# One attention block of three tokens split into two, and the orders of five engines rewritten from the first window sum up to the router

## The chip, the cores and the metric

One core of a Trainium2 chip runs the program. Its engines are TensorE (PE in the profile, with its weight loads as PEld), VectorE (DVE), ScalarE (ACT), GpSimd (POOL) and SyncE (SP), each with its own instruction stream, in order, tied by semaphores. The metric is device time in microseconds (us) of one execution, the median of several.

## What is computed

All in float32. An image tokenizer, an attention layer over 6 tokens, and a mixture of 8 experts with 2 picked for each token, for 64 images:

```python
pe = conv(pixels, conv_w)                     # 6 x 6 patches of 14 x 14 pixels per image, 256 channels
red, win = mean of each 3 x 3 window, its 9 patches      # 4 windows per image
q = ln(red) @ la_wq;  k, v = ln(win) @ la_wkv            # 8 heads of 32, 9 keys each
local = red + softmax(q k) v @ la_proj + la_proj_b       # 4 rows per image
gq = ln(class_emb) @ ga_wq;  gk, gv = ln(local) @ ga_wkv
cls_out = class_emb + softmax(gq gk) gv @ ga_proj + ga_proj_b
h = concat([cls_tok, local @ mod_w + mod_b, cls_out])    # 6 tokens per image: 0, 1 to 4, 5
x = layernorm(h)
h = h + causal_attention(x @ Wq, x @ Wk, x @ Wv) @ Wp + bp   # 16 heads, alibi distances
x = layernorm(h)
logits = x @ gate_w; the two largest, their softmax weights
h = h + sum over both picks of weight * (silu(x @ gate) * (x @ up)) @ down
```

Token i attends to the tokens j <= i, so the attention has 1 + 2 + 3 + 4 + 5 + 6 = 21 pairs.

## The kernel before

The program is one straight order on each engine, written out by hand; what an engine issues waits for semaphores of the others, and everything behind it on that engine waits too.

*The front.* Convolution, window attention (`window_scores`, `score_maximum`, `window_exp`, `window_weights`, `value_products` on two halves wt = 0 and 1). The weighted values of half 0 lie in `vprod` as three groups; `vsum_step` counts the two additions by which GpSimd (L1745) sums them, and `first_aggregate` transposes the sum into `agg0`. Half 1 is summed by TensorE itself in `second_aggregate` (`summed_turn`, L798). `local_rows`, `local_copy`, `local_columns` and `copy_pair` make the `loT` columns of each half.

*From the columns to h.* For each half, `patch_begin` and `patch_rows` (L839, L845) form the rows of h of tokens 1 and 2 (tile 0) and 3 and 4 (tile 1). `global_scores`, a softmax on DVE (L2121 to L2134), `global_value`, `gprod` (L2137), `global_aggregate` (L872), `gaggT` (L2142), `class_begin` and `class_rows` (L886) form those of tile 2, tokens 0 and 5. Each tile's rows get moments (DVE), a reciprocal root (GpSimd, `reciprocal_root`, L1638), the normalised rows `in0`, `in1`, `in2`, a transposition (`turn_in`, L661), a copy to `hT` (ACT), and the products with Wq, Wk, Wv (`qkv`, L958): `qkv_cls` is token 0, `qkv0` tokens 1 and 2, `qkv1` tokens 3 and 4, `qkv_pool` token 5. ACT unpacks each of the four in four copies (`qkv_copy`, L1444 to L1447). h itself is copied to `acc` by ACT (`h_copy`, L1356), and GpSimd adds the bias (`residual`, L1740).

*The token attention.* DVE works in blocks of query tokens (`BLOCKS`): all their query-key products (L517), the sum to scores (`att_dots`, L2062), maximum and difference (`att_scores`), exp on ACT (`attention_exp`, L1452), and sum, reciprocal and product (`att_weights`). A block of queries i0 to i1 works on (i1 - i0) x i1 pairs, masked ones too: 9 and 18, in all 27. `token_values` (L508) multiplies weights and values: GpSimd does tokens 1, 2 and 0, and the keys 0 and 1 of tokens 5 and 3; DVE does the other keys of 5 and 3, and token 4. TensorE transposes and sums (`turn_context`, L798): `ctx0` is tokens 1, 2, 0, `ctx1` tokens 3 and 4, `ctx2` token 5. ACT copies them (L1457), and `out_proj` (L981) adds the product with Wp to h in the banks of the three row tiles.

*Up to the router.* For each tile: moments (`residual_moments`), root, `mid_normalise` (DVE), `turn_mid`, a rounded copy by ACT (`experts_input_hi`, L1463), the rest by DVE (`experts_input_lo`, L2092), and `router`, six matmuls each. `logits_full` is set behind the last. `keep_clock` issues matmuls whose result nobody reads.

*Behind it.* The dense expert (`gate_up`, L1076; `down`, L1086), the picks and the places of the rows (DVE, L2176 to L2259), rows scattered to DRAM and read back, and 11 tiles of 128 rows for the other experts (L1148, L1157, L1171). Expert weights are split in a high and a low part: `weights_hi` and `weights_lo` (GpSimd, L1696) for the dense one, `tile_weights_hi` (L1471) and `tile_weights_lo` (DVE, L2098) in four pieces for each tile. SP loads the second tile's weights (`tile_a(1)`) over the buffers of q, k, v, once all token values are done.

## Time and profile before

| | |
|---|---|
| median of 3 runs | 201.01 us (200.23 to 202.35) |
| the profiled execution | 200.45 us, its span 198.6 us, granted TensorE clock 1.000 |
| busy share of the span | PE 93%, PEld 81%, DVE 70%, ACT 53%, POOL 38% |
| from the window values of half 1 to the logits | 81.5 us to 119.4 us after the span's start |
| from the logits to the last matmul | 119.4 us to 194.5 us |

The span runs from the first to the last instruction. A matmul of float32 operands stands as two in the counts.

### The profile page before, as it was taken

What the parts mean: (1) busy time and instruction counts of PE and PEld (TensorE: products, weight loads), DVE (VectorE), ACT (ScalarE), POOL (GpSimd) and SP (SyncE); (2) the same over time, 40 slices, a digit from 0 to 9 for tenths busy, and PEclk for the clock granted to TensorE, in tenths of its full rate; (3) what the DMA queues carried; (4) which work ended last, traced back from release to release, by engine and by line L of the source; (5) the groups of instructions that cost most, each with busy time, mean ns of one, the idle gap of its engine ahead of it and who ended that gap; (6) DMA issues with size and microseconds to landing.
All of it is one profiled execution on the core that took longest, in us unless ns stands there. A gap on an engine that the chain in (4) does not pass through costs nothing.

```text
span 198.6 us, 3342 instructions
## 1 busy us (share of the span) xinstructions
PE 184.0 (93%) x1093; PEld 160.7 (81%) x1093; DVE 138.6 (70%) x334; ACT 104.8 (53%) x234; POOL 75.2 (38%) x110
## 2 busy tenths in 40 slices
PE   8499999999999999999994879999999999999991
PEld 8499798989798778867892769988888888888880
DVE  1379778095899999857388867938657866766452
ACT  4255477183434646525653254247367877778331
POOL 6105548165635322038835472781000022000770
PEclk9999999999999999999999999999999999999999
DMA  6999999500087000000000490033899999994233
GB/s 193 301 344 337 325 370 317 152 2 0 5 310 323 0 0 3 0 0 2 3 0 0 145 386 0 2 106 93 294 373 381 406 383 373 347 356 147 70 93 79
DMA packets 11933, 34.88 MB, mean 176 GB/s; under 512 B 1462, under 2 KB 7180, under 8 KB 10252
## 3 DMA queue, kind: packets, MB, share of 16 engines
q1 hardware_dynamic: 9436, 30.72, 43.8%
q10 hardware_dynamic: 1904, 2.37, 3.9%
q0 software_dynamic: 576, 1.58, 2.4%
q8 instruction: 9, 0.15, 0.3%
q14 instruction: 8, 0.07, 0.1%
HBM read 30.84 MB, written 3.82 MB: 174 GB/s over the span
## 4 chain that ended last, share of the span: by engine, by line
PE 63%; DVE 22%; issue 4%; DMA 4%; ACT 2%; SPq 2%; POOL 0%; DVEq 0%
PE bank L1148 15%; PE bank L1171 9%; PE bank L616 8%; PE bank L714 4%; PE bank L1076 4%; DMA raw<-xb 4%; PE bank L637 3%; PE bank L1086 3%; PE bank L661 2%; DVE kv_rows L1856 2%; DVE stats L1809 2%; PE bank L1157 2%; DVE vprod L496 2%; SPq L491 1%; DVE window L508 1%
## 5 line engine op out<-in xcount | busy, mean ns | idle before, releaser
L1148 PE MATMUL bank<-split 128*128 128x512 f32 x132 | 33.3, 401 | 0.1
L1148 PEld LDWEIGHTS bank<-split 128*128 128x128 f32 x132 | 24.0, 188 | 5.2 <-DVE split L2270 0.3
L1638 POOL TENSOR_TENSOR rstd<-veps,mhalf 128x1 f32<-128x1 f32 (+2 forms) x17 | 14.3, 842 | 27.7 <-DVE veps L1816 27.6
L616 PE MATMUL bank<-split 128*128 128x256 f32 (+1 forms) x180 | 22.7, 285 | 0.0
L616 PEld LDWEIGHTS bank<-split 128*128 128x128 f32 (+1 forms) x180 | 22.1, 191 | 0.2
L714 PE MATMUL bank<-split 128*128 128x512 f32 x90 | 22.1, 397 | 0.0
L2098 DVE TENSOR_TENSOR split<-raw,split 128x512 fp32r<-128x512 f32 x28 | 18.1, 685 | 4.2 <-ACT split L1471 4.1
L714 PEld LDWEIGHTS bank<-split 128*128 128x128 f32 x90 | 16.4, 188 | 3.3
L1471 ACT CAST split<-raw 128x512 fp32r<-128x512 f32 x28 | 16.6, 619 | 1.8 <-DMA raw<-ffn_w 1.8
L1658 POOL TENSOR_TENSOR window<-window,pe_rows 128x256 f32<-128x256 f32 x14 | 13.3, 951 | 9.0 <-ACT pe_rows L1246 8.3
L1734 POOL TENSOR_SCALAR split<-token_row,window 128x384 fp32r<-128x384 f32 x3 | 4.0, 1349 | 30.7 <-DMA window<-expert_rows 30.7
L2279 DVE TENSOR_TENSOR kv_rows<-bank,kv_rows 128x512 f32<-128x512 f32 x11 | 7.6, 690 | 11.5 <-PE bank L1148 9.5
L637 PE MATMUL bank<-split 128*128 128x256 f32 (+1 forms) x90 | 12.0, 289 | 2.8 <-ACT split L1261 2.8
L1246 ACT COPY pe_rows<-bank 128x256 f32<-128x256 f32 x18 | 6.3, 370 | 15.4 <-PE bank L616 15.4
L1297 ACT ACTIVATE kv_rows<-bank,rstd 128x512 f32<-128x512 f32 x15 | 10.0, 686 | 7.5 <-PE bank L714 6.6
L637 PEld LDWEIGHTS bank<-split 128*128 128x128 f32 (+1 forms) x90 | 11.3, 195 | 3.2 <-ACT split L1261 2.8
...
L2098 DVE TENSOR_TENSOR split<-kv_rows,split 128x512 fp32r<-128x512 f32 x16 | 10.5, 695 | 2.6 <-ACT split L1471 2.6
L1809 DVE BATCH_NORM_STATS2 stats<-pe_rows 128x6 f32<-128x256 f32 x18 | 6.5, 414 | 8.3 <-ACT pe_rows L1246 8.1
L1261 ACT CAST split<-raw 128x384 fp32r<-128x384 f32 (+1 forms) x15 | 6.7, 510 | 8.9 <-DMA raw<-xa 4.6
L1471 ACT CAST split<-kv_rows 128x512 fp32r<-128x512 f32 x16 | 9.5, 620 | 1.4 <-DMA kv_rows<-ffn_w 1.4
L1547 ACT ACTIVATE kv_rows<-bank 128x512 f32<-128x512 f32 x11 | 6.6, 597 | 5.5 <-PE bank L1148 5.5
...
## 6 DMA issues: line engine op xcount, KB each, us to landing
...
```

The source lines that it names most:

```text
L616: mm = pe.matmul(bank[b][:, 0:C], xs[0:n, g % 2, px, a:a + P], cws[0:n, pw, k, :], start=(k == 0 and m == 0), stop=(k == len(KCH) - 1 and ...
L637: mm = pe.matmul(bank[GT * g + j][:, 0:C], xs[0:n, g, px, a:a + P], cws[0:n, pw, k, :], start=(k == 0 and m == 0), stop=last)
L714: mm = pe.matmul(bank[b][:, :], lns[:, g % 2, px, a:a + P], wkvs[:, pw, aw:aw + 2 * C], start=(c == 0 and m == 0), stop=(c == CC - 1 and m ...
L1076: mm = pe.matmul(bank[b][:, 0:NCOL], aws[:, q, pw, a:a + P], ms[:, px, c, FIRST:ROWS], start=(c == 0 and m == 0), stop=(c == CC - 1 and m ...
L1148: mm = pe.matmul(bank[half][:, :], xst[:, s % 2, px, c * P:(c + 1) * P], tile_aws[s % 2][:, piece, pw, :], start=(c == 0 and m == 0), stop ...
L1171: mm = pe.matmul(bank[6][:, 0:C], hcols[s % 2][:, q * P:(q + 1) * P], b_ring[ring(s)][:, q, :], start=(q == 0), stop=(q == FQ - 1))
L1297: act.activation(kv_rows[:, 0:wt + 2:wt + 1, n, :], bank[b][:, :].rearrange("p (k c) -> p k c", k=2), ACT.Identity, scale=rstd[:, k, i - G ...
L1471: act.copy(tile_aws[s % 2][:, piece, HI, :].rearrange("p (q n) -> p q n", q=FQ), a_ring[ring(s)][:, :, piece * P:(piece + 1) * P]).then_in ...
L1638: pool.tensor_tensor(rstd[0:parts, k, 0:n], veps[0:parts, k, 0:n], mhalf[0:parts, 0:n], ALU.pow).then_inc(rstd_done, 1)
L1658: pool.tensor_tensor(redsum[:, wt, :], pe_rows[:, wt, 0, :] if n == 1 else redsum[:, wt, :], pe_rows[:, wt, n, :], ALU.add).then_inc(sum_s ...
L1809: ins = dve.bn_stats(stats[0:parts, j, :], r)
L2098: dve.tensor_tensor(tile_aws[s % 2][:, piece, LO, :].rearrange("p (q n) -> p q n", q=FQ), a_ring[ring(s)][:, :, piece * P:(piece + 1) * P] ...
```

## The change

The attention block of tokens 3, 4 and 5 becomes one of tokens 3 and 4 and one of token 5; all values of tokens 3, 4 and 5 go to DVE. The order of each engine is rewritten: GpSimd's sum of `vprod` goes, TensorE sums the three groups while it transposes; `qkv_cls` is multiplied and copied there, in bank 6 in place of bank 3; `last_keys` goes ahead of `class_keys`; tile 0's rows of h come right behind `local_rows(1)`; DVE adds bias and h (`residual`), in place of an ACT copy and a GpSimd addition; GpSimd's `weights_lo` go elsewhere; `qkv0` and `qkv1` are begun a token at a time; the token values are transposed in the order 4, 5, 3, with `out_proj(2)` between; `router(0)` goes ahead of `turn_mid(1)`; two of DVE's `tile_weights_lo(0, ...)` go behind the last rows, one ahead of and one behind the routing.

The diff, with its lines of context and the declarations of semaphores left out:

```diff
@@ -60,12 +60,11 @@
-BLOCKS = [(0, 3), (3, 6)]
+BLOCKS = [(0, 3), (3, 5), (5, 6)]
 PAIRS = PAIR_AT[-1]
-SHARE = 2
@@ -91,7 +90,7 @@
-QKV = {"qkv_cls": (3, (0,)), "qkv0": (0, (1, 2)), "qkv1": (1, (3, 4)), "qkv_pool": (4, (5,))}
+QKV = {"qkv_cls": (6, (0,)), "qkv0": (0, (1, 2)), "qkv1": (1, (3, 4)), "qkv_pool": (4, (5,))}
@@ -141,10 +140,10 @@
                                                     "loT0", "loT1", "in0", "in1", "in2"],
-    ["conv3", "turn0", "turn1", "turn2", "q0", "turn3", "turn4", "turn5", "gs", "qkv_cls", "ctx0", "mid0"],
+    ["conv3", "turn0", "turn1", "turn2", "q0", "turn3", "turn4", "turn5", "gs", "ctx0", "mid0"],
     ["conv5"] + [f"kv{i}" for i in range(1, TILES, KV_BANKS)] + ["wp2"],
-    ["bv"] + [f"kv{i}" for i in range(2, TILES, KV_BANKS)] + ["wp0"],
+    ["bv"] + [f"kv{i}" for i in range(2, TILES, KV_BANKS)] + ["qkv_cls", "wp0"],
...
@@ -500,14 +499,13 @@
-def token_values(eng, i, j0=0, j1=None):
-    j1 = i + 1 if j1 is None else j1
+def token_values(eng, i):
     x = PAIR_AT[k] + (i - i0) * i1
-    return eng.tensor_tensor(pv[:, pv_at[i] + j0:pv_at[i] + j1, :].rearrange("p j (h e) -> p j h e", e=DV),
-                             v6[:, j0:j1, :, :].rearrange("p j a (g e) -> p j (a g) e", e=DV),
-                             spread(p6[:, x + j0:x + j1, :], 3, DV), ALU.mult)
+    return eng.tensor_tensor(pv[:, pv_at[i]:pv_at[i + 1], :].rearrange("p j (h e) -> p j h e", e=DV),
+                             v6[:, 0:i + 1, :, :].rearrange("p j a (g e) -> p j (a g) e", e=DV),
+                             spread(p6[:, x:x + i + 1, :], 3, DV), ALU.mult)
@@ -557,7 +555,7 @@
         if s == 1:
-            sp.wait_ge(pool_values, BLOCKS[0][1] + 2)
+            sp.wait_ge(pool_values, BLOCKS[0][1])
@@ -787,15 +785,35 @@
+    def qkv(name, part=None):
+        b, tokens = QKV[name]
+        wait_free(pe, b, name)
+        w = QW + KW + VW
+        for n, t in enumerate(tokens):
+            if part in (None, n):
+                for c in range(CC):
+                    mm = pe.matmul(bank[b][:, n * w:(n + 1) * w], hT[:, t, c, :, :].rearrange("p s b -> p (s b)"),
+                                   wqkv[:, c, :], start=(c == 0), stop=(c == CC - 1))
+        if part in (None, len(tokens) - 1):
+            mm.then_inc(filled[b], 1)
+    def summed_turn(out, piece, first, last):
+        return pe.matmul(out, piece, ident, start=first, stop=last, is_transpose=True)
-        pe.wait_ge(vsum_step, 2)
-        for c in range(CC):
-            turn(c, "agg0", [vprod[:, 0, c * P:(c + 1) * P]])
-    def summed_turn(out, piece, first, last):
-        return pe.matmul(out, piece, ident, start=first, stop=last, is_transpose=True)
+        pe.wait_ge(vprod_step, VSTEPS)
+        for c in range(CC):
+            wait_free(pe, c, "agg0")
+            for n in range(GT):
+                mm = summed_turn(bank[c][:, 0:P], vprod[:, n, c * P:(c + 1) * P], n == 0, n == GT - 1)
+            mm.then_inc(filled[c], 1)
+            if c == 0:
+                pe.wait_ge(att_in, 16)
+                pe.wait_ge(tok_cols, 1)
+                qkv("qkv_cls")
@@ -809,7 +827,7 @@
             if k == 0:
-                global_scores(0)
+                local_begin(1)
@@ -890,6 +908,8 @@
         pe.wait_ge(residual_done, ROW_ORDER.index(j) + 1)
+        if j == 2:
+            pe.wait_ge(class_residual, 1)
@@ -933,8 +953,8 @@
     keys_values(GT * 4 + 2)
+    last_keys()
     class_keys()
-    last_keys()
@@ -947,29 +967,22 @@
-    def qkv(name, part=None):
-        b, tokens = QKV[name]
-        wait_free(pe, b, name)
-        w = QW + KW + VW
-        for n, t in enumerate(tokens):
-            if part in (None, n):
-                for c in range(CC):
-                    mm = pe.matmul(bank[b][:, n * w:(n + 1) * w], hT[:, t, c, :, :].rearrange("p s b -> p (s b)"),
-                                   wqkv[:, c, :], start=(c == 0), stop=(c == CC - 1))
-        if part in (None, len(tokens) - 1):
-            mm.then_inc(filled[b], 1)
+    def turn_values(k, b, n):
+        t = CTX_TOKENS[k][n]
+        for j in range(t + 1):
+            mm = summed_turn(bank[b][:, n * P:(n + 1) * P], pv[:, pv_at[t] + j, :], j == 0, j == t)
+        return mm
         wait_free(pe, b, f"ctx{k}")
-        for n, t in enumerate(CTX_TOKENS[k]):
-            for j in range(t + 1):
-                mm = summed_turn(bank[b][:, n * P:(n + 1) * P], pv[:, pv_at[t] + j, :], j == 0, j == t)
+        for n in range(len(CTX_TOKENS[k])):
+            mm = turn_values(k, b, n)
@@ -1005,56 +1018,57 @@
     second_aggregate()
-    local_begin(1)
+    patch_begin(0)
     local_rows(1)
-    global_value(0, 0)
+    patch_rows(0)
     local_columns(1)
-    global_value(0, 1)
+    global_scores(0)
     global_scores(1)
-    patch_begin(0)
-    patch_rows(0)
+    for c in range(CC):
+        global_value(0, c)
     patch_rows(1)
+    class_begin()
+    turn_in(0)
     global_aggregate()
-    class_begin()
+    tile_qkv(0, "qkv0", 0)
     class_rows()
-    turn_in(0)
-    pe.wait_ge(att_in, 16)
-    pe.wait_ge(tok_cols, 1)
-    qkv("qkv_cls")
     turn_in(1)
-    tile_qkv(0, "qkv0", 0)
+    qkv("qkv0", 1)
+    tile_qkv(1, "qkv1", 0)
     turn_in(2)
-    tile_qkv(0, "qkv0", 1)
-    tile_qkv(1, "qkv1")
+    qkv("qkv1", 1)
     wait_copied(pe, 0, "qkv0")
-    keep_clock(0, 6)
+    keep_clock(0, 4)
     turn_context(0, 3)
+    keep_clock(0, 1)
     out_proj(0, [(3, "ctx0")])
+    keep_clock(0, 1)
     pe.wait_ge(dve_values, 1)
-    pe.wait_ge(pool_values, BLOCKS[0][1] + 1)
+    wait_free(pe, 4, "ctx1")
+    turn_values(1, 4, 1)
+    pe.wait_ge(dve_values, 2)
     turn_context(2, 1)
-    pe.wait_ge(pool_values, BLOCKS[0][1] + 2)
+    out_proj(2, [(3, "ctx0"), (1, "ctx2")])
     pe.wait_ge(dve_values, DVE_VALUES)
-    turn_context(1, 4)
-    out_proj(2, [(3, "ctx0"), (1, "ctx2")])
+    turn_values(1, 4, 0).then_inc(filled[4], 1)
+    keep_clock(0, 1)
     turn_mid(0, 3)
-    keep_clock(0, 2)
     keep_clock(0, 1)
-    turn_mid(1, 4)
     router(0, 3)
+    turn_mid(1, 4)
@@ -1336,6 +1350,7 @@
     def in_normalise(j):
+        act.wait_ge(residual_done, ROW_ORDER.index(j) + 1)
@@ -1348,12 +1363,6 @@
         act.copy(lor[:, wt, :], bank[LO_BANK[wt]][:, 0:C]).then_inc(lo_copied, 1)
-    def h_copy(j):
-        act.wait_ge(stats_done, LNS.index(f"in{j}") + 1)
-        rows = slice(0 if j < 2 else B, P)
-        act.copy(acc[rows, j, :], bank[ROW_BANK[j]][rows, 0:C]).then_inc(h_copied, 1)
@@ -1473,9 +1482,11 @@
         aggregate_copy(0, c)
+    act.wait_ge(vprod_step, VSTEPS)
+    qkv_copy("qkv_cls")
     last_values_copy(0)
+    window_exp(1)
     last_values_copy(1)
-    window_exp(1)
@@ -1492,31 +1503,28 @@
     ins.then_inc(gexp_done, 1)
+    in_normalise(0)
     weights_hi(3)
-    h_copy(0)
-    h_copy(1)
-    in_normalise(0)
     hT_copy(0)
-    h_copy(2)
     hT_copy(1)
-    qkv_copy("qkv_cls")
+    qkv_copy("qkv0")
     copy_pair(2, "in2", hT[:, T - 1, :, :, :].rearrange("p c s b -> p c (s b)"))
-    qkv_copy("qkv0")
     tile_weights_hi(0, 0)
+    tile_weights_hi(0, 1)
     attention_exp(1)
-    tile_weights_hi(0, 1)
+    attention_exp(2)
+    context_copy(0, 3)
     tile_weights_hi(0, 2)
-    context_copy(0, 3)
     experts_input_hi(0, 3)
+    experts_input_hi(2, 1)
     token_rows_hi(0)
-    experts_input_hi(2, 1)
@@ -1734,40 +1742,29 @@
-    def residual(j):
-        pool.wait_ge(h_copied, ROW_ORDER.index(j) + 1)
-        pool.tensor_tensor(acc[:, j, :], acc[:, j, :], brow("bp"), ALU.add).then_inc(residual_done, 1)
-    pool.wait_ge(vprod_step, VSTEPS)
-    for n in range(1, GT):
-        pool.wait_ge(vsum_step, n - 1) if n > 1 else None
-        pool.tensor_tensor(vprod[:, 0, :], vprod[:, 0, :], vprod[:, n, :], ALU.add).then_inc(vsum_step, 1)
-    pool.tensor_copy(acc[0:B, 2, :], clsb[0:B, :])
     wait_full(pool, 4 + (TILES - 1) % KV_BANKS, f"kv{TILES - 1}")
+    pool.wait_ge(vprod_step, VSTEPS + GT)
+    weights_lo(0)
+    weights_lo(1)
     reciprocal_root("pool0", 1)
+    pool.tensor_tensor(acc[0:B, 2, :], clsb[0:B, :], brow("bp")[0:B, :], ALU.add).then_inc(class_residual, 1)
     reciprocal_root("pool1", 1)
-    for q in range(GT):
-        weights_lo(q)
     negative_mean("in0")
-    reciprocal_root("in1", 1)
     pool.tensor_tensor(gsplit[:, LO, :, :], gate, gsplit[:, HI, :, :].bitcast(F32), ALU.subtract).then_inc(gate_split, 1)
+    pool.wait_ge(gstep, 5)
+    weights_lo(2)
+    reciprocal_root("in1", 1)
+    weights_lo(3)
     reciprocal_root("in2", 1)
-    residual(0)
-    residual(1)
-    residual(2)
-    weights_lo(3)
     pool.wait_ge(att_step[0], ATT)
+    pool.wait_ge(qk_dve, 2)
         values(t)
-    pool.wait_ge(att_step[1], ATT)
-    token_values(pool, 5, 0, SHARE).then_inc(pool_values, 1)
-    token_values(pool, 3, 0, SHARE).then_inc(pool_values, 1)
@@ -1892,6 +1889,13 @@
         moments(f"in{j}", [bank[ROW_BANK[j]][:, 0:C]])
+    def residual(j):
+        dve.wait_ge(bias_in, 64)
+        rows = slice(0 if j < 2 else B, P)
+        dve.tensor_tensor(acc[rows, j, :], bank[ROW_BANK[j]][rows, 0:C], brow("bp")[rows, :],
+                          ALU.add).then_inc(residual_done, 1)
@@ -2108,8 +2112,9 @@
     local_moments(0)
+    repeat_table()
     local_moments(1)
-    repeat_table()
+    row_moments(0)
@@ -2125,6 +2130,7 @@
     dve.tensor_tensor(gsc[:, :, :], gsc[:, :, :], spread(gm[:, :], 1, 4), ALU.subtract).then_inc(gstep, 1)
+    residual(0)
@@ -2136,40 +2142,43 @@
                       spread(gatt[:, :, :].rearrange("p w h -> p (w h)"), 2, DL), ALU.mult).then_inc(drained[4], 1)
-    row_moments(0)
                       spread(spread(bvg[:, :], 2, 2), 3, B), ALU.add).then_inc(drained[1], 1)
-    dve.wait_ge(h_copied, ROW_ORDER.index(1) + 1)
+    residual(1)
     row_moments(2)
-    dve.wait_ge(h_copied, ROW_ORDER.index(2) + 1)
+    residual(2)
     att_weights(0)
-    attention_products(dve, 1, ("qkv_cls", "qkv0", "qkv1", "qkv_pool")).then_inc(qk_dve, 1)
+    attention_products(dve, 1, ("qkv_cls", "qkv0", "qkv1")).then_inc(qk_dve, 1)
     att_scores(1)
+    attention_products(dve, 2, ("qkv_cls", "qkv0", "qkv1", "qkv_pool")).then_inc(qk_dve, 1)
     att_weights(1)
+    att_dots(2)
+    att_scores(2)
     att_wait(1, ATT)
-    token_values(dve, 5, SHARE, T).then_inc(dve_values, 1)
     values(4)
-    token_values(dve, 3, SHARE, 4).then_inc(dve_values, 1)
+    att_weights(2)
+    att_wait(2, ATT)
+    values(5)
+    values(3)
     residual_moments(0)
+    residual_moments(2)
     mid_normalise(0)
-    tile_weights_lo(0, 0)
-    tile_weights_lo(0, 1)
-    residual_moments(2)
+    mid_normalise(2)
     residual_moments(1)
-    mid_normalise(2)
+    experts_input_lo(0, 3)
     mid_normalise(1)
-    experts_input_lo(0, 3)
     experts_input_lo(1, 4)
+    tile_weights_lo(0, 0)
@@ -2304,6 +2313,7 @@
     hidden(3)
+    tile_weights_lo(0, 1)
```

## Rows read from the trace of the kernel before

**Rows 1.** Page, part 1: busy time, share of the span, instructions.
```profile
PE 184.0 (93%) x1093; PEld 160.7 (81%) x1093; DVE 138.6 (70%) x334; ACT 104.8 (53%) x234; POOL 75.2 (38%) x110
```

**Rows 2.** Chain that ended last, behind the logits: start, duration, what.
```profile
117.23 2.19 PE bank L995 x18
119.42 3.18 PE bank L1076 x21
...
129.20 1.83 PE bank L1086 x8
...
190.99 1.78 PE bank L1171 x8
```

**Rows 3.** The same chain, 99 to 114 us.
```profile
99.77 0.77 DVE vprod L517
...
103.04 1.37 DVE vprod L517
...
108.25 2.61 DVE window L508 x3
...
112.83 1.20 DVE split L2098 x2
```

**Rows 4.** Timeline of PE, 88 to 95 us: start, duration, instruction.
```profile
89.12 1.03 PE L845 MATMUL bank<-tok,loT 128*128 128x256 f32 x4
...
92.14 1.02 PE L872 MATMUL bank<-both_halves,kv_rows 128*128 128x64 f32 x8
...
93.88 1.13 PE L886 MATMUL bank<-tok,gaggT 128*128 128x256 f32 x4 [0.23 <-DVE gaggT L2142]
```

**Rows 5.** Timeline of DVE, 80 to 97 us.
```profile
80.30 0.17 DVE L2103 TENSOR_TENSOR uc<-u,bank 128x16 f32<-128x16 f32 x1
...
96.64 0.54 DVE L1823 TENSOR_SCALAR pe_rows<-bank,mv,rstd 128x256 f32<-128x256 f32 x1 [0.76 <-POOL rstd L1638]
```

**Rows 6.** Timeline of ACT, 98 to 102 us.
```profile
98.59 0.26 ACT L1444 COPY kv_rows<-bank 64x128 f32<-64x128 f32 x1 [0.46 <-PE bank L958]
...
101.62 0.27 ACT L1447 COPY kv_rows<-bank 128x128 f32<-128x128 f32 x1
101.96 0.26 ACT L1452 ACTIVATE kv_rows<-kv_rows 128x72 f32<-128x72 f32 x1
```

**Rows 7.** Groups by shape, DVE, 97 to 120 us: busy, mean ns.
```profile
L508 DVE TENSOR_TENSOR window<-kv_rows 128x640 f32<-128x640 f32 x1 | 1.2, 1242 | 0.0
L508 DVE TENSOR_TENSOR window<-kv_rows 128x256 f32<-128x256 f32 x1 | 0.8, 836 | 0.0
...
L508 DVE TENSOR_TENSOR window<-kv_rows 128x512 f32<-128x512 f32 x1 | 0.7, 691 | 0.0
```

**Rows 8.** Timeline of POOL, parts of 73 to 111 us.
```profile
73.12 2.23 POOL L1745 TENSOR_TENSOR vprod<-vprod 128x256 f32<-128x256 f32 x2 [5.96 <-DVE vprod L501]
...
103.18 2.86 POOL L508 TENSOR_TENSOR window<-kv_rows 128x256 f32<-128x256 f32 x3 [3.36 <-DVE kv_rows L2084]
108.30 2.29 POOL L508 TENSOR_TENSOR window<-kv_rows 128x256 f32<-128x256 f32 x2 [2.27 <-DVE kv_rows L2084]
```

**Rows 9.** Timeline of PE, 105 to 119 us.
```profile
106.09 0.88 PE L798 MATMUL bank<-con,window 128*128 128x128 f32 x6 [1.39 <-POOL window L508]
...
110.97 1.17 PE L798 MATMUL bank<-con,window 128*128 128x128 f32 x9 [0.60 <-POOL window L508]
111.98 1.89 PE L981 MATMUL bank<-att,pe_rows 128*128 128x256 f32 x8
...
116.04 0.44 PE L661 MATMUL bank<-con,pe_rows 128*128 128x128 f32 x2 [1.08 <-DVE pe_rows L1823]
```

**Rows 10.** Timeline of PE from 0 us, and windows (1.00: granted clock).
```profile
9.64 2.53 PE L637 MATMUL bank<-split 128*128 128x256 f32 x19 [2.62 <-ACT split L1261]
...
8.00:10.00 2.00, 0.36 (x3) 0.36 (x4) 0.94 (x2) 0.92 (x3) 0.76 (x3) 1.00 1.06 266
```

**Rows 11.** Timeline of DVE, 127 to 130 us.
```profile
129.07 0.42 DVE L2270 TENSOR_TENSOR split<-bank,split 128x256 fp32r<-128x256 f32 x1 [0.18 <-ACT split L1540]
```

6 lines of the change are left out of this document (3 added, 3 removed).

## The prediction

> **What bounds the kernel now.** I read the busy shares first, then the chain that ended last, then the timelines of the stretch that the diff rewrites. TensorE is busy for 93% of the span [rows 1], but that is a mean of two regimes. Behind the logits, from 119.42 us to 190.99 us and on, the chain is TensorE's matmuls nearly without a break [rows 2]: nothing there becomes shorter by this change, and whatever the logits gain moves through to the end one for one. Ahead of the logits, from 99.77 us on, the chain is VectorE's: the products, the scores, the values, two splits of tile weights, the last rows [rows 3]. There TensorE waits (1.39 us ahead of `ctx0`, 0.60 us ahead of `ctx1`, 1.08 us ahead of a turn) [rows 9]. So the question is when `logits_full` comes, against 119.42 us. I follow the new orders event by event; event times from here on are estimates worked out from the durations of the rows.
>
> **Step 1, the front up to `in2`: 0.0 us (-0.3 to +0.4).** GpSimd loses two additions, 2.23 us [rows 8]; TensorE gets four more transposes (0.11 us each by the 21 of `ctx0` to `ctx2`, of which six take 0.88 us with their tail [rows 9]) and the four matmuls of `qkv_cls`, 224 columns wide, about 0.8 us (eight of 256 columns took 1.89 us [rows 9]). They stand ahead of `last_values` and of the mean of `u`. `uc`, which reads that mean, ran at 80.30 us [rows 5] and went straight ahead of the window weights; it now comes about 0.1 to 0.2 us later, while the weights waited for exp until 80.66 us anyhow. So the wait changes its name and not its time. With `patch_rows(0)` in between, `local_columns(1)` slips by 0.2 us (four matmuls are 0.86 us of array time; 1.03 us with the tail [rows 4], and most of it covers the copy of `lor`). The global softmax gets about that back, since GpSimd no longer works beside it. Tile 0's rows come out 2.5 us earlier (87.5 instead of 90.0 us [rows 4]) but nobody on the chain asks for them. What sets the start of the token attention is tile 2: `global_aggregate` at 92.3 (before 92.14), `class_rows` at 94.0 (before 93.88) [rows 4], then moments, root and the normalised `in2`, which began at 96.64 us after 0.76 us of waiting for the root [rows 5]. DVE's new `residual(2)` fits in that wait. I take 96.7 us. The three `residual` on DVE cost 0.42 us each; `residual(0)` lies under exp of the global softmax, `residual(1)` under the wait for the aggregate's last rows; uncovered they would add 0.8 us, and this is the upper bound of the step.
>
> **Step 2, the first token block: -1.5 us.** Before, its products waited for the last copy of `qkv0` and began at 99.77 us [rows 3]: `qkv_cls` and half of `qkv0` were multiplied and copied behind `in2`. Now both are behind us when `in2` is done (`qkv0` is copied by about 97.2 us), so the products start at 97.25 us, 2.5 us earlier. But exp is queued on ACT behind the copies of `qkv1` and `qkv_pool`, which need `in2`: tile 2's turn at 97.3, the second half of `qkv1` full at 98.4 (before, `qkv0`'s copies began at 98.59 us [rows 6]), 1.1 us for its four copies and 0.8 us for the pool's. These two groups ended at 101.62 + 0.27 us before and end at about 100.4 us now; exp follows at once, as it did at 101.96 us [rows 6]. DVE's scores are ready at 99.4 us and wait a microsecond for it. The second block's products begin at 101.55 instead of 103.04 us [rows 3]: -1.5 us, not -2.5.
>
> **Step 3, two blocks for one, and the values: back to -1.1 us.** The 18 pairs cost 1.37 us of products and 1.50 us of reduction before, and become 10 + 6. By size (9 pairs took 0.77 us [rows 3]) these are 0.84 and 0.92 us for tokens 3 and 4, 0.55 and 0.60 us for token 5; the short instructions (maximum, difference, sum, reciprocal, weights at 0.2 to 0.4 us) are done twice, but each exp is now covered by the other block's work. Values: DVE did 1,408 elements per partition in 2.61 us [rows 3], now it does 1,920, and GpSimd's two (2.29 us [rows 8]) are gone. The price is the disputed point. One instruction of 512 took 691 ns, one of 640 1,242 ns, one of 256 836 ns [rows 7]: the first runs at 1.35 ns an element, the others at twice to four times their share. GpSimd's two ran just then. At the first one's pace 1,920 elements are 2.6 us, at the pace of the other two (2.32 ns) 4.5 us. I take 2.6 us, since GpSimd has done its last value instruction by about 104.4 us, before DVE's first one at 106.75: the new wait on `qk_dve` starts them at 102.4, behind the second block's products, and without being held by them they need some 1.65 us of the 2.86 [rows 8]. They will hold a short DVE instruction or two (0.3 us, in the sum). Put together: weights of tokens 3 and 4 at 105.65, `values(4)` 106.75 to 107.55, `values(5)` done at 109.1, `values(3)` at 109.8, against 110.86 us before.
>
> The Trainium skill says the same as a rule (SBUF — State Buffer, section "Who interferes with whom"): a VectorE instruction with two SBUF inputs and a GpSimd instruction that reads SBUF exclude each other for a whole instruction. By that rule the trace's 1,242 ns are a wait for GpSimd and the work, and the step keeps its 2.6 us; without it one would put 4.5 us and have no gain left.
>
> **Step 4, from the values to the logits: -0.3 us more.** Token 5 is done at 109.1 us; its turn, its copy (0.3 us) and `out_proj(2)` (0.86 us) end at 111.45. Token 3's turn is queued behind `out_proj(2)` and can't use that its values were ready at 109.8; its turn, copy (0.37 us) and `out_proj(1)` end at 113.7 us, which is just where they ended before (111.98 + 1.89 less the tail [rows 9]). So the 1.1 us of step 3 are lost here again. What is new is behind them. Before, DVE put two splits of tile weights (1.20 us [rows 3]) ahead of the moments of tiles 2 and 1, and both last turns (from 116.04 us [rows 9]) stood ahead of 18 router matmuls, 2.19 us [rows 2]. Now the moments of tile 1 run from 113.75 to 114.5, the root (GpSimd) to 115.15, the normalisation to 115.75, the turn to 116.2, ACT's copy and DVE's low part to 117.1. `router(0)` and `router(2)` lie beside that; only the last six matmuls, 0.73 us (a third of 2.19), stand behind. Logits at 118.0 us against 119.42: **-1.4 us** in all.
>
> **Step 5, behind the logits: 0.0 us (0 to +0.6).** One more split (0.6 us, half of the 1.20) stands behind the dense expert's last product and ahead of the first gathered rows, whose low part was done at 129.07 + 0.42 us [rows 11]. The tile's first matmul comes only when `down` ends, 129.20 + 1.83 us [rows 2]: of 1.5 us of cover it uses 0.6. The other split stands ahead of the routing, where DVE waits for the logits. The load of the second tile's weights, queued on SP behind the values, moves a microsecond earlier and has over 10 us to spare.
>
> **The sum.** The profiled execution took 200.45 us, 0.3% under the median. 200.45 - 1.4 = 199.05 us for one like it; 201.01 - 1.4 = **199.6 us** for the median, 0.7% less. About 1%, 2.0 us, is what a measurement of this kernel can tell from no change.
>
> **The rivals.**
> - *TensorE's clock falls: slower.* The granted clock is 1.00 all through, and the longest pause through which it held is 2.62 us, in a stretch with 0.36 us of matmuls in 2 us [rows 10]. The change has pauses of about 2.2 us (102.2 to 104.4) and 2.0 us (105.5 to 107.5), with single `keep_clock` between, and fewer matmuls in all there. If that brings 1.2 GHz in place of 2.4 from 105 us on, the work on the chain doubles: turns 0.66 + 0.44 + 0.22, projections 2 x 0.86, routers 1.46 us, together 4.5 us. 201.01 - 1.4 + 4.5 = 204.1 us; if it comes back midway, about 202. It decides from a clock under 1.00 in any window from 102 to 118 us. Against it: both pauses are shorter than the one that held.
> - *The blocks' overhead eats the gain: no change.* If the third block's short instructions and the contended pace cost 1 to 2 us more than step 3 says, `ctx2` is a microsecond late and everything behind it: 201.01 - 0.4 = 200.6 us.
> - *More than the sum: faster by over 1%.* If `in2` comes 0.5 us sooner (GpSimd is out of DVE's way between 73 and 75 and between 89 and 92 us) and the copies behind it keep pace, and DVE's short instructions run without being held, `out_proj(2)` is not at 111.45 but 110.6: 198.6 us.
> - *It doesn't do what it says:* router and rows overlap only if `mid1` is late enough; if tile 1's path is shorter than I think, the routers queue and 0.7 us are left behind. This stays inside the range, 200.3 us.
>
> **How the numbers follow.** The sum with its near neighbours 0.45, more than the sum 0.30, overhead or queue 0.16, clock 0.09. The range reaches from a gain of 3.0 us (198.0) to a loss of 0.8 us (201.8), which leaves out most of the clock's case and a sliver of the fast one. Faster by over 1% means under 199.0: 0.33; slower by over 1% means over 203.0: 0.07; 0.60 within.
>
> **What would show it.** Step 1: `in2` normalised on DVE near 96.7 us. Step 2: DVE idle about 1 us ahead of the first sum of weights, ended by ACT's exp, and the second products near 101.5. Step 3: values of 640, 768 and 512 elements near 0.8, 1.0 and 0.7 us, the last ending near 109.8. Step 4: the last `out_proj` still near 113.7, but six router matmuls alone behind the last turn, logits near 118.0. Step 5: all later events 1.4 us earlier and TensorE without a new gap at tile 0. The prediction is wrong if `in2` moves by over half a microsecond, if the values run at 2 ns an element, or if the clock leaves 1.00.

## The result, and the profile after

The changed kernel takes 199.32 us (median of 20 runs, 197.37 to 202.15), the kernel before 200.25 us beside it (20 runs, 199.49 to 202.35). The ratio is 0.9897 (95% interval 0.9865 to 0.9929): 1.0% faster. That ratio compares the means of the fast executions alone, within 1.5% of each kernel's fastest, and so leaves out 8 of the 20 of the changed kernel and none of the kernel before. By all executions the change is worth less: the means differ by 1.03 us (199.50 against 200.53, 0.5%), the medians by 0.93 us. A mean granted clock of at least 0.998 was recorded in 11 of 32 executions of the changed kernel (with its repetition and the first edit below) and in 14 of the 57 of the kernel before that came with a clock; the 20 of the kernel before named here came without one.

The profiled execution took 201.53 us (span 199.6) and is one of the longer ones. Its front is not disturbed; behind the logits it has a stall of its own, and its clock line shows where:

```profile
PE 185.7 (93%) x1095; PEld 162.5 (81%) x1095; DVE 140.3 (70%) x344; ACT 104.1 (52%) x232; POOL 70.3 (35%) x103
...
PEclk9999999999999999999999999999987999999999
```

The first line answers to [rows 1]: GpSimd has 5 us less, DVE and TensorE 1.7 us more. TensorE's 1.7 us come from a stretch at a lower clock shown below; in after_a3, without one, it is busy for 184.0 us, as before.

Events of two executions can't be compared by their time from the span's start. I count from DVE's instruction on the class query (`gqc`, at 72.96 us before and 72.11 us after), which lies ahead of everything that the diff changes on the chain; over the traces of this case it comes at 71.1 to 73.9 us. All times "after the mark" below are differences to it.

| us after the mark | before | forecast | after |
|---|---|---|---|
| `in2` normalised, start | 23.68 | 23.7 | 23.75 |
| first products, start | 26.81 | 24.3 | 24.38 |
| first exp, start | 29.0 | 27.4 | 27.26 |
| second products, start | 30.08 | 28.6 | 28.32 |
| values end | 37.90 | 36.8 | 36.23 |
| last `out_proj`, end | 40.9 | 40.7 | 40.3 |
| logits read by DVE | 46.49 | 45.0 | 44.75 |

One difference in the table is measured unevenly: the forecast for the last `out_proj` leaves out the tail of its last matmul, which the measured 40.9 and 40.3 hold.

DVE's timeline after, for [rows 3], [rows 5] and [rows 7] (start, duration, instruction, the idle time ahead of it and what ended it):

```profile
79.50 0.17 DVE L2107 TENSOR_TENSOR uc<-u,bank 128x16 f32<-128x16 f32 x1 [0.68 <-PE bank L772]
...
95.86 0.54 DVE L1820 TENSOR_SCALAR pe_rows<-bank,mv,rstd 128x256 f32<-128x256 f32 x1 [0.23 <-POOL rstd L1646]
96.49 0.76 DVE L515 TENSOR_TENSOR vprod<-kv_rows 128x576 f32<-128x576 f32 x1
...
99.67 0.24 DVE L2083 TENSOR_REDUCE d<-kv_rows 128x24 f32<-128x72 f32 x1 [1.03 <-ACT kv_rows L1461]
...
100.43 0.82 DVE L515 TENSOR_TENSOR vprod<-kv_rows 128x640 f32<-128x640 f32 x1
...
105.30 0.82 DVE L506 TENSOR_TENSOR window<-kv_rows 128x640 f32<-128x640 f32 x1
...
106.78 1.56 DVE L506 TENSOR_TENSOR window<-kv_rows 128x768 f32<-128x768 f32 x2
```

The products follow `in2` at once, and DVE then stands for 1.03 us for exp. ACT shows why: exp is right behind the last copy of token 5, as before [rows 6]:

```profile
99.21 0.27 ACT L1456 COPY kv_rows<-bank 128x128 f32<-128x128 f32 x1
99.37 0.28 ACT L1461 ACTIVATE kv_rows<-kv_rows 128x72 f32<-128x72 f32 x1
```

The groups by shape, DVE, 97 to 120 us (busy, mean ns): every value instruction goes at 1.25 to 1.34 ns an element. GpSimd's three took 2.86 us before [rows 8] and now 1.78:

```profile
L506 DVE TENSOR_TENSOR window<-kv_rows 128x768 f32<-128x768 f32 x1 | 1.0, 959 | 0.0
L506 DVE TENSOR_TENSOR window<-kv_rows 128x640 f32<-128x640 f32 x1 | 0.8, 818 | 0.0
L506 DVE TENSOR_TENSOR window<-kv_rows 128x512 f32<-128x512 f32 x1 | 0.7, 684 | 0.0
```

```profile
101.39 1.78 POOL L506 TENSOR_TENSOR window<-kv_rows 128x256 f32<-128x256 f32 x3 [5.58 <-DVE vprod L515]
```

DVE's own values are no longer on the chain that ended last. Before, they were [rows 3]; now the chain runs from the scores of token 5 to ACT's third exp (L1461), the copy of `ctx0` (L1466), which stands behind that exp in ACT's queue, the projection of tile 0, the turns of tokens 4 and 5 in one piece, and the projection of tile 2:

```profile
105.42 0.24 ACT kv_rows L1461
105.66 0.38 ACT pe_rows L1466
...
106.08 1.13 PE bank L994 x4
107.21 0.43 PE bank L1016 x2
107.64 1.22 PE bank L803 x11
...
108.88 0.27 ACT pe_rows L1466
...
109.29 1.12 PE bank L994 x4
```

`ctx0`'s turn is over at 104.09 us and ACT is idle from 103.21 to 105.42 us, but the copy has its place behind the third exp.

TensorE, for [rows 9]: two pauses of 1.80 and 1.55 us ahead of `ctx0`'s turn and its projection, then the projections apart, and behind the last turn 12 router matmuls (`router(2)` and `router(1)`, of which the last six are on the chain) instead of 18 behind all turns:

```profile
103.22 0.87 PE L803 MATMUL bank<-con,window 128*128 128x128 f32 x6 [1.80 <-POOL window L506]
103.94 0.60 PE L1016 MATMUL bank<-att,con 128*128 128x256 f32 x2
106.08 1.13 PE L994 MATMUL bank<-att,pe_rows 128*128 128x256 f32 x4 [1.55 <-ACT pe_rows L1466]
...
111.29 1.13 PE L994 MATMUL bank<-att,pe_rows 128*128 128x256 f32 x4
...
114.56 0.44 PE L659 MATMUL bank<-con,pe_rows 128*128 128x128 f32 x2
114.89 1.93 PE L1008 MATMUL bank<-gsplit,split 128*128 128x168 f32 x12
```

Behind the logits this execution needs 82.74 us to its end, the one before 79.15. The chain that ended last names the cause: the load of the fourth routed tile's weights is queued on SP behind the wait for the scattered rows, and ACT's split, DVE's product and TensorE wait for it:

```profile
132.15 2.80 DMA expert_rows<-pe_rows,dest_row
...
137.57 7.49 DMA raw<-ffn_w
...
145.08 0.63 ACT split L1480
...
147.08 0.66 PE bank L1171 x4
147.74 4.36 PE bank L1162 x12
```

TensorE pauses 1.91 us there, and behind the pause the granted clock is under 1.00 in two windows, from 148 to 155 us (span, busy time and instructions of PE, PEld, DVE, ACT, POOL, then the clock): at 1.2 GHz in part of both, so that 12 matmuls take 4.36 us instead of the 2.77 us of an undisturbed tile.

```profile
146.00:148.00 2.00, 0.92 (x6) 0.88 (x7) 2.00 (x5) 2.00 (x6) 0.00 (x0) 1.00 0.97 389
148.00:150.00 2.00, 2.00 (x7) 1.57 (x7) 1.97 (x6) 1.79 (x5) 0.00 (x0) 0.62 0.96 369
150.00:155.00 5.00, 5.00 (x23) 4.06 (x22) 2.94 (x6) 3.06 (x8) 0.00 (x0) 0.81 1.01 357
```

### The profile page after: what moved, and what is told of

It is laid out like the page before. It is cut to its first block, busy times and chain, and to the rows that moved or that the text cites. A ratio compares the mean times of both kernels' runs of the same rounds, so it can differ in the third digit from the quotient of the medians.

```text
span 199.6 us, 3350 instructions
## 1 busy us (share of the span) xinstructions
PE 185.7 (93%) x1095; PEld 162.5 (81%) x1095; DVE 140.3 (70%) x344; ACT 104.1 (52%) x232; POOL 70.3 (35%) x103
## 4 chain that ended last, share of the span: by engine, by line
PE 60%; DVE 15%; DMA 8%; issue 5%; POOL 3%; SPq 3%; ACT 3%; DVEq 0%; POOLq 0%
PE bank L1162 12%; PE bank L614 8%; PE bank L1185 8%; PE bank L712 6%; DMA raw<-ffn_w 4%; DMA raw<-xb 3%; PE bank L635 3%; POOL expert_rows L1734 3%; DVE stats L1806 2%; PE bank L1171 2%; PE bank L803 2%; PE bank L659 2%; PE bank L723 2%; PE bank L1090 2%; DMA expert_rows<-pe_rows,dest_row 1%
## 5 line engine op out<-in xcount | busy, mean ns | idle before, releaser
L1162 PE MATMUL bank<-split 128*128 128x512 f32 x132 | 34.9, 415 | 0.1
L1162 PEld LDWEIGHTS bank<-split 128*128 128x128 f32 x132 | 25.0, 196 | 5.4 <-DVE split L2279 0.3
L712 PE MATMUL bank<-split 128*128 128x512 f32 x90 | 22.1, 397 | 0.0
L712 PEld LDWEIGHTS bank<-split 128*128 128x128 f32 x90 | 16.5, 188 | 3.2
L1742 POOL TENSOR_SCALAR split<-token_row,window 128x384 fp32r<-128x384 f32 x3 | 5.8, 1943 | 34.0 <-DMA window<-expert_rows 33.9
L1704 POOL TENSOR_TENSOR split<-raw,split 128x512 fp32r<-128x512 f32 x4 | 5.0, 1270 | 18.1 <-DVE vprod L495 16.9
```

Source lines behind the costliest of these rows:

```text
L712: mm = pe.matmul(bank[b][:, :], lns[:, g % 2, px, a:a + P], wkvs[:, pw, aw:aw + 2 * C], start=(c == 0 and m == 0), stop=(c == CC - 1 and m ...
L1162: mm = pe.matmul(bank[half][:, :], xst[:, s % 2, px, c * P:(c + 1) * P], tile_aws[s % 2][:, piece, pw, :], start=(c == 0 and m == 0), stop ...
```

## The experiments

**The fourth tile's load, alone in both kernels.** In both kernels SP issues `tile_a(3)` behind the scattered rows. The edit puts it ahead of that wait:

```diff
             tile_a(2)
+            tile_a(3)
             sp.wait_ge(scattered, PICKS * RT * 16)
             for s in range(GATHERED, ROW_RING):
                 tile_rows(sp, s)
-            tile_a(3)
```

*before_a3*, the kernel before with this edit: 

> The kernel before, with one load moved: the fourth routed tile's gate and up weights (tile_a(3)) are issued ahead of SP's wait for the scattered rows, in place of behind it and the four row loads. Theory A (the load is late by its place in SP's queue, and the kernel before has about 1 us of cover for it): its weights land before 136 us in place of 145.5, and the time stays the same, within 0.3% (200.0 to 200.6 us on a base of 200.25), since nothing waited; the scatter of different executions narrows. Theory B (the DMA engines are the bound of this stretch, the load is late wherever it is issued): the rows or the next loads come later by as much and the time grows by 0.5 us or more.

Measured: 200.40 us (6 runs), ratio to the kernel before 0.9977 (0.9937 to 1.0016); logits at 46.38, from there to the end 79.55 us. The kernel before gains nothing that can be measured, as theory A has it; the profile of the unedited kernel before shows a near tie there: ACT waited 1.80 us for that load (until 145.52 us), DVE's product that hangs on it ended at 147.46, and TensorE came for it at 147.67 us.

*after_a3*, the changed kernel with it: 

> The changed kernel with the same load moved. Theory A: the changed kernel brings TensorE to the fourth tile 1.8 to 2.6 us earlier but the load, which hangs on the scattered rows and lands after 7.5 us, not; with the load early the pause ahead of the tile's hidden turn (1.9 us) and the stretch at half clock behind it (1.6 us) go away: 197.6 to 198.4 us in nearly every execution, 1% or more under the kernel before, and no granted clock under 1.00. Theory B (the clock falls because of the pauses before the router, or the rows land late too): times still spread from 197 to 202 us.

*after_again*, the changed kernel once more, unedited, on the same chip: 

> The changed kernel unchanged, for a second profile beside the same base. Both theories: logits near 1.8 us earlier than in the kernel before, counted from the sum of the window values. Theory A: where the fourth tile's weights land early enough the profile is short (195.5 to 197 us of span) and shows no pause there; where they land late it is long and shows it.

Measured: after_a3 198.89 us, ratio 0.9907 (0.9857 to 0.9957); after_again 199.01 us, 0.9911 (0.9860 to 0.9962). The edit is worth nothing in the median, and the times still spread from 197.87 to 200.98 us: theory B. In after_a3's trace there is no pause and the clock holds in the same windows; to the end it needs 79.12 us, as long as the kernel before. But after_again has no pause at the fourth tile either: the stall of the first profile belongs to some executions. Its own disturbance is elsewhere, behind the pauses ahead of the projections (the timeline of TensorE, then windows):

```profile
105.99 1.83 PE L994 MATMUL bank<-att,pe_rows 128*128 128x256 f32 x4 [1.55 <-ACT pe_rows L1466]
```

```profile
104.00:106.00 2.00, 0.45 (x4) 0.05 (x2) 1.91 (x6) 0.68 (x3) 0.00 (x0) 1.00 0.00 0
106.00:110.00 4.00, 4.00 (x15) 3.37 (x16) 2.82 (x9) 0.45 (x1) 0.70 (x2) 0.57 0.23 35
```

The same four matmuls take 1.83 us instead of 1.13, the granted clock of 106 to 110 us is 0.57, and the logits come at 46.41 us after the mark instead of 44.75: 1.66 us for this fall. Up to that place the events of the table agree within 0.01 us with those of the first profile. What decides in which execution the clock falls, these runs don't show.

**The first exp ahead of the copies of token 5** (*after_a3_exp*, on top of after_a3):

```diff
-            qkv_copy("qkv_pool")
             attention_exp(0)
+            qkv_copy("qkv_pool")
```

> after_a3 with one more edit: ACT computes exp of the first token block ahead of the four copies of token 5's projection (qkv_pool). In the changed kernel DVE waits 1.03 us for this exp, which is queued behind the copies of qkv1 and qkv_pool. Theory (step 2 of the prediction: ACT's queue sets the second block's start): exp starts 0.6 us earlier, just behind qkv1's copies, the values end 0.5 us earlier and the time falls by 0.3 to 0.5 us. Rival (behind the values the order of TensorE's projections sets the end): less than 0.2 us.

Measured: exp at 26.59 us after the mark (0.67 earlier), second products at 27.64 (0.69 earlier), values end at 35.55 (0.68 earlier). So ACT's queue was what held the blocks, as step 2 has it. The time is 198.80 us, ratio 0.9895 (0.9854 to 0.9935), no better than after_a3: the 0.3 to 0.5 us that were expected don't show. The profiled execution is again one whose clock fell, for longer (0.57 from 106 to 108 us, 0.50 from 108 to 113), with the logits at 46.70. With this edit and no fall they would be at about 44.1 (44.75 less the 0.68 us), so this fall cost about 2.6 us. Ahead of it the projection of tile 0 starts 0.68 us earlier too (33.29 instead of 33.97).

**More matmuls over the pauses** (*warm*, on top of after_a3; *before_warm*, the kernel before with `tile_a(3)` ahead and 9 in place of 6 and 3 more):

```diff
-            keep_clock(0, 4)
+            keep_clock(0, 8)
             pe.wait_ge(pool_values, BLOCKS[0][1])
             turn_context(0, 3)
-            keep_clock(0, 1)
+            keep_clock(0, 4)
```

> after_a3 with more matmuls whose result nobody reads, in the two pauses ahead of the projections: keep_clock(0, 8) in place of 4 ahead of the context of tokens 1, 2 and 0, and 4 in place of 1 behind its turn. They fill 1.8 and 1.5 us of waiting and delay nothing that is on the chain. Theory (in some executions the clock falls to the lower level in these pauses, which costs 1.8 us each time): the granted clock is 1.00 from 98 to 118 us in every execution, the median falls from 198.9 to 198.0 to 198.3 us and the spread shrinks. Rival (the falls come from elsewhere, from the start of the kernel or from loads): the spread stays and the median is within 0.2 us of after_a3.

> before_a3 with the same filling: keep_clock(0, 9) in place of 6, and 3 more behind the first context's turn. Theory: the kernel before has falls of the clock in its own pauses (104.7 to 106.1 and 106.8 to 108.6 us) too, so its median falls to 199.7 to 200.0 us; against warm this leaves the change alone, at one clock: 1.7 to 2.1 us. Rival (only the changed kernel falls): it stays at 200.4 and the change is worth more, 2.3 us.

Measured: warm 198.96 us (12 runs), ratio 0.9989 (0.9956 to 1.0021); before_warm 199.91 us (12 runs), 1.0014 (0.9977 to 1.0051). The kernel before took 199.61 us beside them (35 runs). The gain that was expected does not show: warm's median is not under that of after_a3 (198.89 us, on another chip), before_warm's is 199.91 us as expected but not under its base, and the two lie 0.95 us apart, not 1.7 to 2.1. The mean clocks of warm were 0.989 to 0.999, and its executions lie closer together (all but two within 198.75 to 199.33). At the logits warm is where after is, 44.76 us, but to its end it needs 80.02 us instead of 79.12, and so it gives back part of what it saves. Its last chain is not TensorE's but GpSimd's: the last rows written to DRAM (`far_out`) land late, the gathers from them start late, and DVE adds them late. In after_a3 that write took 4.6 us (issued at 176.74, first gather at 181.31); in warm, issued at the same distance from the mark (104.6 us), it took 6.0 us (175.75 to 181.75). The profiles of all six variants of the changed kernel with the added matmuls show an end of this length (79.86 to 80.17 us behind the logits), those of after_a3 and after_a3_both (79.12) don't. But the added matmuls are not all of it: before_warm has them and a short end (write 4.6 us, end 79.20 us), before_a3 does not have them and a write of 5.6 us and an end of 79.55 us. Why the write lands later stays open.

**One block again** (*warm_blocks2*: tokens 3, 4 and 5 in one block, all values on DVE, the rest as in warm):

```diff
-BLOCKS = [(0, 3), (3, 5), (5, 6)]
+BLOCKS = [(0, 3), (3, 6)]
...
-            attention_products(dve, 2, ("qkv_cls", "qkv0", "qkv1", "qkv_pool")).then_inc(qk_dve, 1)
```

> warm with the split of the attention block undone: tokens 3, 4 and 5 are one block of 18 pairs again, all their values on DVE behind its weights; every other order as changed. Prediction's step 3: the two blocks cost about what the one does (0.84 + 0.55 and 0.92 + 0.60 us of long work for 1.37 + 1.50) and hide one exp, and token 5's chain is what the next step waits for: the one block is 0.1 to 0.5 us slower. Rival (the third block's short instructions are pure overhead): it is 0.3 us or more faster.

Measured: 198.38 us, ratio 0.9931 (0.9897 to 0.9964). Its DVE timeline beside that of after above:

```profile
102.19 1.36 DVE L515 TENSOR_TENSOR vprod<-kv_rows 128x1152 f32<-128x1152 f32 x1
...
106.26 0.41 DVE L2082 TENSOR_REDUCE d<-kv_rows 128x24 f32<-128x144 f32 x1 [0.39 <-ACT kv_rows L1461]
...
107.39 2.29 DVE L506 TENSOR_TENSOR window<-kv_rows 128x640 f32<-128x640 f32 x3
```

The values end at 35.82 us after the mark, 0.42 sooner than with the two blocks: the third block's short instructions cost more than the one wait for exp (0.39 us) that they cover. The projections begin within 0.13 us of those of warm and the logits are at 44.78. So no gain of the split, which gives the change its name, shows at the logits. The time is 0.58 us less than warm's in the median on the same chip, where 0.1 to 0.5 us more was expected; the one profile, an execution with a stretch of low clock at its start (0.66 in 10 to 15 us), does not show where that comes from.

The added matmuls blur this comparison. In warm_blocks2 the copy of `ctx0` is done at 106.92 us, but the projection of tile 0 starts only at 107.97 us, behind the matmuls without a reader that follow the turn. Without the added ones it could start up to a microsecond earlier (an estimate, the difference of these two times), and one block would be ahead of two; no run tried it.

**Both edits of order** (*warm_both*: warm, the exp as above, and token 3's turn ahead of `out_proj(2)`; *after_a3_both*: the same two on after_a3, without added matmuls):

```diff
-            out_proj(2, [(3, "ctx0"), (1, "ctx2")])
             pe.wait_ge(dve_values, DVE_VALUES)
             turn_values(1, 4, 0).then_inc(filled[4], 1)
+            out_proj(2, [(3, "ctx0"), (1, "ctx2")])
```

> warm with two edits: exp of the first token block ahead of qkv_pool's copies on ACT, and token 3's turn ahead of out_proj(2) on TensorE. Theory (both queues stand on the chain, as steps 2 and 4 say): 0.5 us from the first, 0.3 to 0.5 us from the second, together 0.6 to 1.0 us under warm, 197.3 us. Rival (the tail hangs on tile 2's rows as much as on tile 1's): the second gives nothing since it delays out_proj(2) by 0.4 us, and the sum is 0.3 to 0.5.

> The changed kernel with three edits and without added matmuls: the fourth tile's load issued ahead of SP's wait for the scattered rows, the first exp ahead of the copies of token 5 on ACT, token 3's turn ahead of the projection of token 5. Theory: logits 44.0 us after the mark where the clock holds (0.77 earlier than the changed kernel, as in warm_both against warm), but the gathers of the rows from DRAM at the end take part of it, and the clock falls in some executions: median about 198.3 us, 0.3 us under the changed kernel and 1.1% under the kernel before. Rival: without the added matmuls the pauses before the projections bring the clock down in most executions, as in after_a3_exp: no gain over the changed kernel, ratio 0.99 to the kernel before, logits at 45.5 or later.

Measured: logits at 43.99 us (warm_both) and 43.98 us (after_a3_both) after the mark, 0.77 earlier than with the change alone. Nearly all of it is the exp: the projection of tile 2 starts 0.69 us earlier (36.50 instead of 37.19 in warm), as the values end 0.69 us earlier. Token 3's turn now fits in TensorE's wait for the copy of `ctx2`, and the last projection starts 1.32 us earlier, but DVE takes tile 1 behind tile 2 and starts its moments only 0.75 us earlier. So the second edit is worth under 0.1 us: the rival, that the tail hangs on tile 2's rows as much, was right, though `out_proj(2)` is not delayed. warm_both takes 198.20 us, 0.9948 (0.9923 to 0.9973), 0.76 us less than warm in the median (0.9 us more than the 197.3 that was expected), still with the late write at its end (80.05 us behind the logits); after_a3_both 197.78 us beside 200.89 us of the kernel before, 0.9888 (0.9825 to 0.9952), and 79.12 us behind the logits. One of its six executions lasted 307.3 us at a granted clock of 0.56 and is no part of the ratio. Its three executions at full clock have a mean of 197.2 us; after_a3's three, on another chip, 198.0.

**What in step 4 pays** (both on warm). *warm_splits_back* puts two splits of tile weights back between tile 0 and the moments of tile 2:

```diff
             residual_moments(0)
-            residual_moments(2)
             mid_normalise(0)
+            tile_weights_lo(0, 0)
+            tile_weights_lo(0, 1)
+            residual_moments(2)
             mid_normalise(2)
...
             experts_input_lo(1, 4)
-            tile_weights_lo(0, 0)
...
             hidden(3)
-            tile_weights_lo(0, 1)
```

> Two splits of the first tile's weights, which the change took out of the stretch before the logits, go back to where they stood before it: behind the moments and the normalisation of tile 0, ahead of the moments of tile 2. Everything else as in warm. Theory: this is the part of step 4 that pays. The splits take 1.2 us of DVE; about 0.4 us of that fits into DVE's wait for the projection of tile 2 (1.34 us, of which the root and the normalisation of tile 0 take 0.9), so the moments of tiles 2 and 1 come about 0.8 us later and so do the last turn and the logits: 45.4 to 45.7 us after the mark against 44.76 in warm. Rival: the last projection is what the logits wait for, not DVE; then the logits stay within 0.1 us of 44.76.

Measured: logits at 45.65 us, 0.89 later, the upper end of what was expected. The moments of tile 2 start at 39.31 instead of 38.33 us and wait for the splits alone:

```profile
110.49 1.28 DVE L2102 TENSOR_TENSOR split<-raw,split 128x512 fp32r<-128x512 f32 x2
111.69 0.42 DVE L1806 BATCH_NORM_STATS2 stats<-bank 128x6 f32<-128x256 f32 x1
```

*warm_router_back* puts all 18 router matmuls behind the last turn:

```diff
-            router(0, 3)
             turn_mid(1, 4)
+            router(0, 3)
             router(2, 1)
```

> The router matmuls of tile 0 go back behind the turn of tile 1, so that all 18 stand behind the last turn. Everything else as in warm. Theory: the last turn ends at the same time; behind it TensorE then has 12 matmuls (1.45 us) while ACT and DVE make both parts of tile 1 (0.9 us from the turn's end), so the last six start 0.5 us later: logits 45.2 to 45.3 us after the mark against 44.76. Rival, as step 4 of the prediction counts it, 12 matmuls leave the tail and each one counts: 0.73 us later, 45.5 us. Second rival: they lie in the wait wholly and cost nothing, 44.8 us.

Measured: logits at 45.06 us, 0.30 later, between the 0.5 us of the theory and the nothing of the second rival. TensorE now goes through without a gap, and most of the first 12 lie in the time that ACT and DVE need for tile 1:

```profile
114.22 0.41 PE L659 MATMUL bank<-con,pe_rows 128*128 128x128 f32 x2 [1.36 <-DVE pe_rows L1820]
114.39 2.22 PE L1008 MATMUL bank<-gsplit,split 128*128 128x168 f32 x18
```

**GpSimd beside DVE** (*warm_pool_beside*): GpSimd's three value instructions are held until DVE has the second block's weights.

```diff
-            pool.wait_ge(qk_dve, 2)
+            pool.wait_ge(att_step[1], ATT)
```

> GpSimd's three value instructions wait until DVE has the weights of tokens 3 and 4, so that they run beside DVE's values, as in the kernel before. Everything else as in warm. Theory: the two engines shut each other out for whole instructions: of DVE's three instructions of 640, 768 and 512 elements at least two take over 1.2 us in place of 0.82, 0.96 and 0.68, and GpSimd's three last about 2.7 us or more in place of 1.8; values end 1 to 2 us later than the 36.2 us of warm. ctx0 comes late too (its values start some 4 us later), so the logits are 1.5 to 3 us later. Rival: the long instructions of the kernel before were long for another reason (their slices of keys, or the copies of ACT beside them); then DVE's take 0.82, 0.96 and 0.68 us here too, and only ctx0 is late.

Measured: the pattern as expected, the sizes not. GpSimd ran at its own pace, and was done before most of DVE's values began, so only what stood beside it shows the price, and it is on DVE alone: GpSimd's three took 1.77 us and not 2.7. Its timeline, then DVE's:

```profile
104.35 1.77 POOL L506 TENSOR_TENSOR window<-kv_rows 128x256 f32<-128x256 f32 x3 [8.38 <-DVE kv_rows L2088]
```

```profile
104.12 0.60 DVE L2066 TENSOR_REDUCE kv_rows<-vprod 128x48 f32<-128x432 f32 x1
104.75 0.24 DVE L2072 TENSOR_REDUCE m<-kv_rows 128x8 f32<-128x48 f32 x1
105.02 0.81 DVE L2075 TENSOR_TENSOR kv_rows<-kv_rows,m 128x48 f32<-128x48 f32 x1
105.75 1.05 DVE L506 TENSOR_TENSOR window<-kv_rows 128x640 f32<-128x640 f32 x1
```

The two reductions, with one input, take what they take in warm (0.59 and 0.24 us). The subtraction of 48 elements, with two, takes 0.81 instead of 0.21 us, the values of 640 elements 1.05 instead of 0.82; the other two, behind GpSimd's end, 959 and 687 ns as ever. The values end 0.54 us later (1 to 2 were expected). The projection of tile 0 is 4.0 us late and with it the logits, 48.69 us, 3.9 later. Not all of that is the order: GpSimd starts 2.81 us later (32.10 instead of 29.29), and behind TensorE's pause of 2.87 us the granted clock fell (0.54 in 106 to 108 us, 0.60 in 108 to 110), in spite of the added matmuls, so that the turn and the eight matmuls ahead of the projection take 1.54 and 2.92 us instead of 0.87 and 1.89.

## Why the prediction was right, step by step

The forecast was 199.6 us for a gain of 1.4 us from the logits on. Measured: 199.32 us, and 1.74 us at the logits. That the time agrees to 0.3 us is partly luck, since two misses cancel. The forecast stood on a median of 201.01 us from three runs, 0.76 us over that of twenty; and the medians differ by 0.93 us, 0.47 less than the forecast. The gain itself depends on what is compared: 0.93 us by the medians, 1.03 by the means of all executions, 2.1 by the ratio. On the chip of after_a3 it is 1.8 us by the medians of all executions (200.72 of 11, 198.90 of the 12 of after_a3 and after_again) and 1.85 by the means at a clock of at least 0.998 (199.91 of 2, 198.06 of 6). There both kernels lose about as much to executions at a lower clock (0.8 us each in the median), so these don't explain why the first comparison shows only 0.93; that stays open.

*Step 1 held.* `in2` moved by 0.07 us (forecast 0.0). `uc` stands behind the mean of `u` with a wait of 0.68 us and starts at 7.39 us after the mark against 7.34 before. The wait is longer than the one for exp that it replaces (0.19 us), because DVE's scores are done 0.66 us earlier: `gqblk` alone takes 0.57 us less without GpSimd's sum beside it. This gain, which the step does not count, is lost again in the wait for TensorE.

*Step 2 held, term by term.* Products 2.43 us earlier (2.5), DVE's wait for exp 1.03 us (a microsecond), second products 1.76 us earlier (1.5). That the wait is ACT's queue is shown by after_a3_exp.

*Step 3: the disputed pace was right, the sum 0.6 us too cautious.* Values take 2.46 us on DVE (forecast 2.6). The alternative, 4.5 us, is out: the rule of the Trainium skill that was weighed (SBUF — State Buffer, "Who interferes with whom") agrees with warm_pool_beside, where DVE's instructions with two inputs are held beside GpSimd and those with one are not. The reading of [rows 7] was not exact: the instructions of 640 and 256 elements took 1.4 and 2.4 times their share, not twice to four times. The values end 1.67 us earlier, not 1.1: 0.3 more from step 2, 0.14 from the values themselves, and 0.2 from the instructions between them. Those that GpSimd held cost 0.31 us, as put down (0.36 and 0.75 us against 0.24 and 0.56 in warm_pool_beside). But the step has a flaw that the runs lay open: the split of the block shows no gain. warm_blocks2 ends its values sooner and has the same logits, though with the added matmuls in between. What made the values shorter is that GpSimd no longer works beside them, and what made them sooner is step 2.

*Step 4: right in sum, wrong in what is waited for.* It takes token 5's values as the start of the path. They were ready at 107.74 us (106.78 + 0.96), but TensorE was at their turn only at about 108.2 us (107.64 and five matmuls of token 4 at 0.11 us each), and the path runs from the third exp on ACT to the copy of `ctx0` and the projection of tile 0. That `out_proj(2)` was forecast nearly right (38.5 us after the mark, measured 38.3 with its tail) is luck in this respect. Nor does the last `out_proj` decide alone: it ends about 0.6 us earlier than before (40.3 instead of 40.9 us), and at the same time, within 0.1 us, DVE comes from tile 2's rows to the moments of tile 1; warm_both has the projection 1.3 us earlier than warm and these moments only 0.75. What the logits gain is seen at two places. The moments of tile 1 start 1.38 us earlier (40.35 instead of 41.73 us): 0.89 us of it is what the two splits cost when they go back, the remaining 0.5 us no run takes apart. And from there to the logits it takes 0.36 us less, 4.40 instead of 4.76: that is the first router (0.30 us by its return, not the 0.73 us of six matmuls).

*Step 5 held for what it looked at.* Without a disturbance 79.12 us behind the logits against 79.15. What it did not look at is the fourth tile's load. It counted the cover of the second's (over 10 us) and not that of the one queued behind the scattered rows, which had 0.2 us in the kernel before (147.67 less 147.46). In the first profile the load landed 28.2 us behind the logits instead of 26.1: issued 1.1 us later by the logits (0.8 us because SP's four row loads ahead of it took 2.56 instead of 1.75 us, 0.3 us because they began later), and 7.5 us long instead of 6.5. 2.1 less 0.2 is the pause of 1.91 us; with the fall of the clock behind it the end came 3.6 us later. A bound of +0.6 us for this step was too low.

*The rivals.* "TensorE's clock falls" came about, in a part of the executions: its place was right (106 to 110 us, behind pauses of 1.80 and 1.55 us, for which 2.2 and 2.0 us were forecast), its condition was met in after_again and after_a3_exp, and its price was 1.66 us in the one and about 2.6 in the other, around the lower value put down (from 199.6 to about 202) and not 4.5, since the clock came back in between. The argument against it, that both pauses are shorter than the one of 2.62 us that held [rows 10], is refuted: pauses of under 2 us were followed by a fall in one execution and not in the next. Its chance of 0.09 was meant for all executions or none, which is not how it behaves. "More than the sum" was right at the logits (1.74 for 1.4 us), but not by its reason, since `in2` did not come sooner: GpSimd was out of DVE's way, and the wait for the mean of `u` took that back. Overhead of the blocks exists (0.42 us at the end of the values) but is not on the path to the logits in warm. "Router and rows don't overlap" is out.

What is shown: ACT's queue ahead of the first exp, that GpSimd holds DVE's instructions with two inputs, what the two parts of step 4 cost when they go back (each in one execution on warm), the price of two falls of the clock. What is read from the chain and not tested alone: ACT's queue ahead of the copy of `ctx0`; no run puts that copy ahead of the third exp. What stays open: what the split of the block is worth without added matmuls, what decides in which execution the clock falls, why the gain in time was 0.93 us on one chip and 1.8 on another, and why the last rows land later in some variants.
